# Narrow blocks of a graph kernel: the column halves of TensorE take alternate contraction tiles

## The reference

```python
# layer 0, two hops
for k in range(2):
    agg = adj @ x
    x = tanh(concat([agg, x], axis=1) @ W[k])
# layer 1
adj @ (x @ weight) + bias
# layer 2
adj @ (x * (u >= 0.1) / 0.9)
# layer 3
deg = adj.sum(axis=1, keepdims=True)
concat([x, adj @ x / (deg + 1.0)], axis=-1) @ W.T
```

## Time and profile before

| | |
|---|---|
| median of 3 runs | 2271.01 us |
| profiled execution, its own time | 2271.1 us |
| its span, first to last instruction | 2269.3 us |
| PE busy | 2242.2 us, 99% |
| PEld busy | 1046.0 us, 46% |
| DVE busy | 1253.0 us, 55% |
| ACT busy | 116.4 us, 5% |
| HBM read | 822.31 MB, 363 GB/s over the span |
| granted TensorE clock | full in every slice |

### The profile page before, as it was taken

One profiled execution on the slowest core, in us unless ns is written; L12 is line 12 of the kernel. 1 busy time (PEld: TensorE's weight loads), 2 busy tenths in 40 slices (PEclk: granted clock), 3 DMA queues, 4 the chain that ended last, 5 costly groups with the idle time before them and its releaser, 6 DMA issues.

```text
span 2269.3 us, 32806 instructions
## 1 busy us (share of the span) xinstructions
PE 2242.2 (99%) x13886; PEld 1046.0 (46%) x13886; DVE 1253.0 (55%) x2612; ACT 116.4 (5%) x240; POOL 9.6 (0%) x22
## 2 busy tenths in 40 slices
PE   6999999999999999999999999999999999999999
PEld 3555555555555444444453333333444444444446
DVE  7133222224777399987879888877534322222226
ACT  1000000000002211100100000000000000000000
POOL 0000000000000000000000000000000000000000
PEclk9999999999999999999999999999999999999999
DMA  9999999999999878788988888886999999999997
GB/s 398 421 421 412 401 401 397 383 387 397 397 409 371 293 284 325 299 301 308 358 298 335 324 328 319 315 338 249 347 375 408 406 409 408 407 407 407 408 406 313
DMA packets 116866, 826.56 MB, mean 364 GB/s; under 512 B 13808, under 2 KB 15984, under 8 KB 16752
## 3 DMA queue, kind: packets, MB, share of 16 engines
q1 hardware_dynamic: 112752, 820.04, 91.7%
q0 software_dynamic: 768, 2.10, 0.3%
q10 hardware_dynamic: 3200, 2.33, 0.3%
HBM read 822.31 MB, written 2.10 MB: 363 GB/s over the span
## 4 chain that ended last, share of the span: by engine, by line
PE 97%; DMA 2%; DVE 1%; ACT 0%; issue 0%; ACTq 0%; DVEq 0%
PE double_acc L746 59%; PE single_acc L720 17%; PE spare L746 14%; PE spare L720 6%; DMA ring<-in_adj 2%; PE natural L802 1%; DMA resid<-in_x 0%; DVE centred L933 0%; DVE resid L1147 0%; DVE stats L921 0%; DVE partial L989 0%; DVE partial L1052 0%; DVE moments L924 0%; PE spare L814 0%; ACT L841 0%
## 5 line engine op out<-in xcount | busy, mean ns | idle before, releaser
L746 PE MATMUL double_acc<-ring,operand 128*64 128x512 f32 x6176 | 1350.6, 592 | 0.4 <-DVE operand L1141 0.2
L746 PEld LDWEIGHTS double_acc<-ring,operand 128*64 128x64 f32 x6176 | 477.1, 137 | 790.4 <-issue 773.9
L720 PE MATMUL single_acc<-ring,operand 128*64 128x256 f32 x3472 | 411.6, 382 | 20.4 <-DVE operand L947 11.8
L989 DVE TENSOR_TENSOR partial<-spare,partial 64x256 f32<-64x256 f32 (+1 forms) x204 | 107.0, 525 | 495.6 <-PE spare L746 273.6
L720 PEld LDWEIGHTS single_acc<-ring,operand 128*64 128x64 f32 x3472 | 276.4, 138 | 172.8 <-issue 76.8
L746 PE MATMUL spare<-ring,operand 128*64 128x512 f32 x1456 | 330.4, 592 | 0.6 <-DMA ring<-in_adj 0.6
L970 DVE TENSOR_TENSOR deg_part<-deg_part,ring 128x1024 f32<-128x1024 f32 x215 | 263.3, 1225 | 7.4
L969 DVE TENSOR_TENSOR deg_part<-deg_part,ring 128x1024 f32<-128x1024 f32 x215 | 263.1, 1224 | 6.4
L746 PEld LDWEIGHTS spare<-ring,operand 128*64 128x64 f32 x1456 | 125.7, 137 | 149.1 <-issue 141.5
L989 DVE TENSOR_TENSOR partial<-single_acc,partial 64x256 f32<-64x256 f32 x118 | 49.8, 422 | 174.1 <-PE single_acc L720 172.2
L720 PE MATMUL spare<-ring,operand 128*64 128x256 f32 x1152 | 134.2, 379 | 0.0
(11 more groups left out here) (64 smaller groups left out, 576.8 us busy)
## 6 DMA issues: line engine op xcount, KB each, us to landing
ring<-in_adj SPq DMA_DIRECT2D x766, 1024.0 KB, 7.6
held<-in_adj SPq DMA_DIRECT2D x12, 1024.0 KB, 9.4
kept<-in_adj SPq DMA_DIRECT2D x2, 1024.0 KB, 13.0
for_layer<-in_u POOLq DMA_DIRECT2D x16, 128.0 KB, 2.4
out_rows<-resid ACTq DMA_DIRECT2D x16, 128.0 KB, 6.2
resid<-in_x SPq DMA_DIRECT2D x2, 512.0 KB, 6.0
resid<-in_x SPq DMA_DIRECT2D x1, 1024.0 KB, 13.3
w_stack<-in_w_both ACTq DMA_DIRECT2D x2, 32.0 KB, 7.1
```

Of the source, the lines that this page charges most:

```text
L720: last = nc.tensor.matmul(acc[half_of(h), 0:HALF], operand[:, b.j * TPB + t, half_of(b.row.half)], stream[:, t, nodes_of(h)], start=b.firs ...
L746: last = nc.tensor.matmul(acc[half_of(half), :], operand[:, b.j * TPB + t, half_of(half)], stream[:, t, :], start=b.first and t == 0, stop ...
L989: return nc.vector.tensor_tensor(to, got, to, ALU.add)
```

## The change

`one_product` no longer gives each column half its own 256 output nodes. The column halves take the contraction tiles in turn: tile 0 and 2 go to the first, 1 and 3 to the second, each over all 512 nodes. A narrow block is 4 matmuls of 512 columns in place of 8 of 256. Each PSUM half then holds, for all 512 nodes, the sum over half of the contraction, so the two halves have to be added: `take_added` and `take_first` issue two 64 x 512 instructions, the second on the result of the first, with `link` between. `by_tiles` is true for both kinds of narrow block.

```diff
+def by_tiles(row, kind):
+    return kind in ("single", "late")
...
             def one_product(b, acc):
                 stream = tiles_of(b)
+                if by_tiles(b.row, b.kind):
+                    for t in range(TPB):
+                        last = nc.tensor.matmul(
+                            acc[half_of(t % 2), :], operand[:, b.j * TPB + t, half_of(b.row.half)], stream[:, t, :],
+                            start=b.first and t < 2, stop=b.last and t >= TPB - 2)
+                    return last
                 for t in range(TPB):
                     for h in range(2):
...
                     got = single_acc[row.r % 2]
-                    for h in range(2):
+                    by = by_tiles(row, "single")
+                    if by:
+                        if HELD_OVER[row.r]:
+                            link(nc.vector.tensor_tensor(stacked, got[half_of(0), :], partial[part, row.i, :], ALU.add))
+                        else:
+                            link(nc.vector.tensor_copy(stacked, got[half_of(0), :]))
+                        last = nc.vector.tensor_tensor(stacked, got[half_of(1), :], stacked, ALU.add)
+                    for h in range(0 if by else 2):
...
                 got = bank_of(("taken", last.number))
-                for h in range(2):
+                by = by_tiles(row, "late")
+                if by:
+                    to = partial[half_of(row.half), row.i, :]
+                    link(add_to(to, got[half_of(0), :], ("added", count, row.sweep) in FRESH))
+                    adding = add_to(to, got[half_of(1), :], False)
+                for h in range(0 if by else 2):
```

## The result

The changed kernel takes 2280.66 us (median of 5 runs, 2278.81 to 2280.76) against 2271.03 us (2270.99 to 2271.11): slower by 9.6 us, ratio 1.0041 (95% interval 1.0030 to 1.0051). The profiled execution took 2280.76 us, span 2279.0 us.

The account below looks back on a forecast made before the run. TensorE was taken as the bound, with 97% of the chain of waits. Waits of 2.1 + 2.7 + 2.45 + 3.4 = 10.65 us, less 2.5 us streaming, gave +8.15 and 2279.2 us for the median, range 2274.4 to 2282.8 us.

Parts of the forecast that it names:

- Streaming: TensorE's narrow blocks: 1.717 us each, from 1.726; 263 blocks at 0.0095 us, 2.5 us less.
- rivals C and D: C: larger fixed cost per pass, takes covered, 2265.2 us, chance 0.03; D: halves no longer overlap, 2790 us, chance 0.02.
- A take is 0.56 us longer: VectorE, each narrow group: two dependent 64x512 adds take 1.42 us, where two 64x256 adds took 0.86.
- rival E: Takes at the bounds: 0.40 us more each gives 2275.4 us, 0.65 gives 2281.5; within the forecast's chance of 0.86.
- Turn 1 to 2: Sweep 1 to 2: four longer takes less 0.13 us slack, 2.1 us of waiting at the post of row 14.
- Turn 2 to 3: Sweep 2 to 3: post of row 1 2.55 us late, another 0.1 at the block needing its operand; together 2.7 us.
- roomy: Places outside the turns and last rows: banks needed later, one take a row in sweeps 2 and 3; no waits counted.
- Turn 3 to 4: Sweep 3 to 4: the post waits 1.85 us, the operand ends 2.45 late for a block already waiting; 2.45 us.
- a sign of being wrong: The forecast is wrong if PE waits elsewhere, such as for a bank in the last third; no size given.
- Last rows: End of sweep 5: VectorE's delay grows at the posts that wait for takes, up to the last post; 3.4 us.
- Sum: Whole kernel: 10.65 us of waits less 2.5 us streaming, +8.15 on 2271.1 us: 2279.3, median 2279.2 us.
- Rival B: Takes stay covered at the turns, nothing is lost and the streaming gain stays: 2268.1 us, chance 0.09.

Follow-up runs that it names:

- covered: The changed kernel with the new form only for lates of sweep 5 and singles of sweep 1 up to row 13, old form elsewhere: 2268.82 us.
- single_only: The changed kernel with only the singles in the new form, the lates in the old form: 2272.74 us (six runs of 2272.6 to 2272.7, five of 2274.2).
- filler: The changed kernel with 6 more 64 x 512 matmuls, result unused, on TensorE ahead of the post of row 8 in the last rows: 2278.77 us.
- padded: The kernel before with one more VectorE instruction (64x352, 0.52 us) ahead of each take of a narrow group: 2282.95 us.
- after_turn: The changed kernel with the last row's turned features moved from row 9 to the start of sweep 5, after row 15's first block: 2275.97 us.

## Why the prediction was right, and where its sizes were off

- **Streaming.** 9 to 10 ns a block were forecast; covered shows 9.8. Nothing larger came, so rivals C and D are out: halves with other weights and another stream overlap as the rest.
- **A take is 0.56 us longer.** 1.41 against 0.86 in the rows, 0.55. The 0.04 us for a dependent pair, read at the scaled rows, holds here too (2250.23 + 0.68 to 2250.95). So neither bound of rival E came.
- **Turn 1 to 2.** Forecast 2.1 us at the post of row 14. Measured 2.0 us there and 0.1 at the post of row 15, counted as time without streaming beyond the usual pitch of passes.
- **Turn 2 to 3.** Forecast 2.7 us, nearly all at the post of row 1. The rows show 0.34 us at the post of row 0, 0.39 at the first wide block and 1.46 at the post of row 1, together 2.2; the working named no wait at the first two. It had VectorE 0.5 us late at row 0's part; against a TensorE that is itself 0.82 us later there, the rows show 0.3. Another 0.5 us came at two posts that the working called roomy, in sweep 3 at 1197 and 1217 us, 0.26 and 0.24. There a row's sum stands behind degree sums, and the extra length of the takes ahead had pushed these back. VectorE and the post at the first (changed kernel):

```profile
1196.15 0.69 DVE L993 TENSOR_REDUCE deg_quarter<-deg_part 128x16 f32<-128x512 f32 x1
1196.75 0.67 DVE L1090 TENSOR_TENSOR stack<-double_acc,partial 64x512 f32<-64x512 f32 x1
...
1197.48 0.69 PE L814 MATMUL natural<-w_stack,stack 128*64 128x64 f32 x16
```

The same sum and post in the kernel before:

```profile
1193.11 0.67 DVE L1071 TENSOR_TENSOR stack<-double_acc,partial 64x512 f32<-64x512 f32 x1
...
1194.16 0.64 PE L802 MATMUL natural<-w_stack,stack 128*64 128x64 f32 x16
```

There the sum ended 0.38 us ahead of the post, here 0.06 us, which is the time of a release. So "there is one take a row" was no reason for room, and that the total of 2.7 came out is luck: 0.5 too much at the turn, 0.5 missing in sweep 3.
- **Turn 3 to 4.** Forecast 2.45: measured 0.23 at the late that uses spare again, 1.6 at the post, and 0.56 more at the block that waited before: 2.4. The row of the first names no releaser; a bank still being taken fits, as the take ahead ended at 1600.05 and the late started at 1600.20. The working had said that banks have room and had named a wait for one as a sign of being wrong. It is small, and part of the wait that would have come at the post.
- **Last rows.** Forecast 3.4 us. Without slow issue and drop of the clock (single_only) it is 1.2 + 1.3 + 0.5 = 3.0 us more at the three posts that wait. In four of five executions of the changed kernel some 1.9 us come on top; in the profiled one they are 0.56 from the issue and 1.4 from the clock. This is the term that was missing: the working ended the price of a wait at the wait.
- **Sum.** The streaming gain is 263 blocks at 9.8 ns, 2.6 us. 2.1 + 2.7 + 2.4 + 3.0 - 2.6 = 7.6 us on the profiled 2271.1, which is 2278.7 us, the level of the fastest run (2278.81) and of filler (2278.77). With 1.9 on top it is 2280.6, the median within 0.1. The forecast of 2279.2 lies between the two levels: its mechanism, a longer take where VectorE's queue is full, made 10.2 us of waits of the 10.65 forecast, and the clock was not in it.
- **Rival B** (takes stay covered) fell: the 0.13 us of room were what the rows said. But covered shows that its condition can be met by choosing the blocks.
- **The clock at the start.** Its column says full in every slice, and the working took it so. The first 20 passes of the kernel before took 631 ns each at the median, where the group's is 379:

```profile
L720 PE MATMUL single_acc<-ring,operand x20: 631/631/686, 11.8 to 15.7; 128*64 128x256 f32 x20
```

631 ns is also the length of padded's passes of the same shape from 2255 to 2257 us, at a share of 0.50. So TensorE starts at 1.2 GHz in spite of the column. The changed kernel's first passes are slow as well (up to 1112 ns, its median 592), so the comparison is little touched.

## What to carry to other kernels

An engine that is busy 55% can still set the time at a few places. Look for the places where its queue runs without a gap up to something the bounding engine waits for; there an instruction costs its full length times the number ahead, and elsewhere next to nothing: 87 us more work on VectorE made some 10 us of waits. A change that trades a little of the bounding engine's time for more of another's should be made block by block: here the same edit gives 2.25 us in 246 blocks (230 of them not waiting for a load), and the kernel is 9.6 us slower than before if the 74 others are included. A wait that grows can cost more than its length, as here, where TensorE's clock fell behind the longest one.

## What the runs showed of the hardware

- TensorE's clock fell to 1.2 GHz behind 3.4 us without streaming and stayed there for about 3.4 us: two narrow blocks took 4.81 us in place of 3.6, and 1.4 us were lost net. It also fell behind 2.9 us (padded) and did not behind 2.8 us in one execution of single_only, whose runs have two levels 1.5 us apart. With 2.6 us of unneeded matmuls in the wait, or with the wait gone (after_turn), no execution of 5 and of 11 shows a drop.
- Issues of the same output transfer by ScalarE took 0.34 us or 0.90 us, in executions of kernels that are the same up to there.
- A matmul pair whose halves differ in weights and in stream has the pitch of the wide blocks' pairs: 3.44 us for 8 pairs over 512 columns, where a wide block takes 3.43.
